# Up-product sums scaled out of PSUM by ScalarE, with the bias added by GpSimd, in place of one VectorE operation

## The reference

```python
# x = x + read(layernorm(x), ctx_1024)
q = query @ Wq.T + bq;  k = mem_state @ Wk.T + bk;  v = mem_state @ Wv.T + bv
scores = einsum('btd,bsd->bts', q, k) / sqrt(256)
# all but the 32 largest scores of a row are set to -inf
ctx = softmax(masked) @ v;   return ctx @ Wo.T + bo
# x = x + ffn(layernorm(x))
def bitlinear(x, w, b):
    xq = act_quant(rmsnorm(x))      # rounded to 8 bits by the row's largest value
    wq = weight_quant(w)            # rounded to -1, 0, 1 times the mean size
    return einsum('bsd,fd->bsf', xq, wq) + b
h = gelu(bitlinear(h, w1, b1));  return bitlinear(h, w2, b2)     # 256 -> 1024 -> 256
```

## Time and profile before

| | TensorE | VectorE | ScalarE | GpSimd |
|---|---|---|---|---|
| busy of the 300.1 us span | 278.8 | 242.7 | 207.7 | 128.4 |
| share | 93% | 81% | 69% | 43% |

### The profile page before, as it was taken

The page is one execution under the profiler, slowest core; times in us unless marked ns, Lnnn a source line. Parts: engine busy times, 40 slices in busy tenths (PEclk is TensorE's granted clock), DMA queues, the critical chain, the costliest instruction groups (busy, mean ns, idle before and its releaser), DMA issues. The chain is left out here.

```text
span 300.1 us, 5613 instructions
## 1 busy us (share of the span) xinstructions
PE 278.8 (93%) x1640; PEld 243.7 (81%) x1640; DVE 242.7 (81%) x1000; ACT 207.7 (69%) x319; POOL 128.4 (43%) x211
## 2 busy tenths in 40 slices
PE   7999998999999999999999999999999989959735
PEld 7989997998778977898789888978897879838424
DVE  2563799798889988998899888998897888965761
ACT  1559586355489658965896579667976697474871
POOL 4025773603924292529342935194419131504020
PEclk9999999999999999999999999999999999998957
DMA  7971010001000101010101010101000100100001
GB/s 238 303 272 37 3 35 1 21 0 52 4 17 0 56 0 52 3 54 2 54 0 55 1 52 2 54 3 52 2 20 0 54 2 18 36 2 1 32 3 37
DMA packets 12461, 12.25 MB, mean 41 GB/s; under 512 B 3597, under 2 KB 11342, under 8 KB 12430
## 3 DMA queue, kind: packets, MB, share of 16 engines
q1 hardware_dynamic: 11726, 10.83, 11.2%
q0 software_dynamic: 272, 0.79, 1.2%
q10 hardware_dynamic: 432, 0.26, 0.3%
HBM read 9.77 MB, written 2.10 MB: 40 GB/s over the span
## 5 line engine op out<-in xcount | busy, mean ns | idle before, releaser
L393 PE MATMUL bank<-vo,pT 128*128 128x257 f32 (+1 forms) x416 | 98.3, 385 | 0.0
L393 PEld LDWEIGHTS bank<-vo,pT 128*128 128x128 f32 (+1 forms) x416 | 77.2, 192 | 10.7 <-issue 0.2
L1352 DVE MAX8 cand<-s_sb 128x8 f32<-128x50 f32 (+1 forms) x512 | 62.0, 201 | 5.8 <-ACT s_sb L999 5.6
L999 ACT ACTIVATE s_sb<-score 128x400 f32<-128x400 f32 x64 | 31.5, 501 | 28.7 <-PE score L241 28.7
L241 PE MATMUL score<-k_high,q_low 128*128 128x400 f32 (+1 forms) x128 | 50.7, 396 | 0.0
L241 PE MATMUL score<-k_low,q_high 128*128 128x400 f32 (+1 forms) x128 | 44.2, 346 | 0.0
L241 PE MATMUL score<-k_high,q_high 128*128 128x400 f32 (+1 forms) x128 | 44.1, 344 | 0.0
L1049 ACT ACTIVATE pT<-bank 128x512 f32<-128x512 f32 x64 | 32.9, 516 | 12.5 <-PE bank L249 12.5
L249 PE MATMUL bank<-ident,e_all 128*128 128x128 f32 (+1 forms) x208 | 33.0, 275 | 8.1 <-ACT pT L1049 6.9
L249 PEld LDWEIGHTS bank<-ident,e_all 128*128 128x128 f32 (+1 forms) x208 | 24.7, 141 | 15.0 <-issue 11.2
L1387 DVE SCALAR_TENSOR_TENSOR e_all<-s_sb,best,e_all 128x1601 f32<-128x1601 f32 x16 | 32.5, 2033 | 3.1 <-ACT e_all L1041 3.1
(11 more groups left out here) (141 smaller groups left out, 529.9 us busy)
## 6 DMA issues: line engine op xcount, KB each, us to landing
x_in<-in_x SPq DMA_DIRECT2D x16, 128.0 KB, 2.2
w_sb<-in_L_ffn_w SPq DMA_DIRECT2D x2, 1024.0 KB, 14.3
x_res<-in_x SPq DMA_DIRECT2D x16, 128.0 KB, 2.0
out<-o_sb SPq DMA_DIRECT2D x16, 128.0 KB, 2.0
ctx_sb<-in_ctx SPq DMA_DIRECT2D x3, 512.0 KB, 5.6
b_bc<-in_L_ffn_b POOLq DMA_DIRECT2D x1, 512.0 KB, 9.3
w_q<-in_L_xattn_Wq SPq DMA_DIRECT2D x1, 256.0 KB, 3.0
w_k<-in_L_xattn_Wk ACTq DMA_DIRECT2D x1, 256.0 KB, 4.7
```

The lines of the kernel that those rows point to most:

```text
L393: ins = pe.matmul(bank[:, 0:DV], pT[0:n, t % 2, b * P:(b + 1) * P], vo[0:n, b, :], start=(b == 0), stop=(b == SB - 1))
L999: act.activation(s_sb[:, t % 2, at:at + n], score[c][:, 0:n], ACT.Copy).then_inc(s_copied, 1)
L1352: ins = dve.max(cand[:, t % 2, k:CAND:PIECES], s_sb[:, t % 2, k * PIECE:end])
```

## The change

`hidden` moves from VectorE to ScalarE. There it is an activation with a scale for each row, without the bias. A new GpSimd step `add_bias` adds the bias in place, and `gelu` waits for that by a new semaphore `biased` instead of for the bank. 32 operations leave VectorE, 32 come to ScalarE and 32 to GpSimd. The bank of `up` is free once ScalarE has read it.

```diff
@@ -853,6 +823,12 @@
                 pool.tensor_tensor(row2[:, t // 2 % 2, 1, u:u + 1], row2[:, t // 2 % 2, 0, u:u + 1], minus_half[:, 0:1],
                                    ALU.pow).then_inc(last2_step[u], 1)
 
+            def add_bias(t, h):
+
+                u, part = t % 2, slice(h * BANK, (h + 1) * BANK)
+                wait_drained(pool, ("up", t, h))
+                pool.tensor_tensor(g[:, u, part], g[:, u, part], b1_bc[:, part], ALU.add).then_inc(biased, 1)
...
@@ -1063,10 +1043,22 @@
                 take(("y1", t), y1T[:, :, u * P:(u + 1) * P], two_parts(("y1", t))[:, :, u * P:(u + 1) * P],
                      bias=unmagic_col[:, 0:1])
 
+            def hidden(t, h):
+
+                j, u = t // 2, t % 2
+                if t < LAST:
+                    act.wait_ge(row1_step, (j + 1) * ROW1)
+                else:
+                    act.wait_ge(last1_step[u], ROW1)
+                if t >= 2:
+                    act.wait_ge(y2_ready, t - 1)
+                src = wait_full(act, ("up", t, h))
+                drain(act.activation(g[:, u, h * BANK:(h + 1) * BANK], src[:, :], ACT.Copy, scale=row1[:, j % 2, 6, u:u + 1]),
+                      ("up", t, h))
+
             def gelu(t):
 
-                for h in range(2):
-                    wait_drained(act, ("up", t, h))
+                act.wait_ge(biased, 2 * t + 2)
                 act.activation(g[:, t % 2, :], g[:, t % 2, :], ACT.Gelu).then_inc(g_ready, 1)
 
             def squares(t):
...
@@ -1509,19 +1508,6 @@
                 dve.wait_ge(g_max_ready, t + 1)
                 tile_scales(row2, t // 2 % 2, u, last2_step[u], g_max[:, u:u + 1], wmean[:, 1:2])
 
-            def hidden(t, h):
-
-                j, u = t // 2, t % 2
-                if t < LAST:
-                    dve.wait_ge(row1_step, (j + 1) * ROW1)
-                else:
-                    dve.wait_ge(last1_step[u], ROW1)
-                if t >= 2:
-                    dve.wait_ge(y2_ready, t - 1)
-                src = wait_full(dve, ("up", t, h))
-                drain(dve.scalar_tensor_tensor(g[:, u, h * BANK:(h + 1) * BANK], src[:, :], row1[:, j % 2, 6, u:u + 1],
-                                               b1_bc[:, h * BANK:(h + 1) * BANK], ALU.mult, ALU.add), ("up", t, h))
-
             def gelu_max(t):
 
                 u = t % 2
@@ -1561,115 +1547,126 @@
```

The calls of all engines are put in a new order. The diff of these lists is long; a few of its lines stand here, of GpSimd's round:

```diff
+            for r in range(7):
+                if live(r - 1):
+                    residual(2 * r - 2)
+                if live(r):
+                    split_queries(r)
+                if live(r - 1):
+                    residual(2 * r - 1)
+                if live(r - 2):
+                    add_bias(2 * r - 4, 0)
+                    add_bias(2 * r - 4, 1)
+                    add_bias(2 * r - 3, 0)
...
+                    keep_residual(r - 2, 1)
+                    add_bias(2 * r - 3, 1)
```

More of the change, by code:

```diff
@@ L486, in _ @@
             scores(1, 2)
[L487 to L492, removed]
+            for r in range(7):
+                if r == 0:
+                    project_values(6)
+                if live(r):
+                    scores(2 * r + 1, 3)
+                if live(r - 2):
+                    turn_y2(2 * r - 3, 0)
+                    turn_y2(2 * r - 3, 1)
+                    down(2 * r - 4)
+                if live(r):
+                    turn_weights(2 * r, 0)
                 if live(r - 2):
@@ L520, in _ @@
                 if live(r + 1):
-                    scores(2 * r + 2, 2)
+                    scores(2 * r + 2, 3)
                 if live(r):
@@ L1633, in _ @@
                 if live(r):
-                    best_8(2 * r + 1, 0)
-                    next_8(2 * r + 1, 1)
                     next_8(2 * r + 1, 2)
-                if live(r + 2):
-                    ln1_stats(r + 2)
-                if live(r):
                     next_8(2 * r + 1, 3)
+                    count(2 * r + 1)
+                    attended(2 * r)
+                    weigh(2 * r + 1)
+                    largest_count(2 * r + 1)
+                    release(2 * r + 1)
+                    moments(2 * r)
+                if live(r + 1):
+                    candidates(2 * r + 2, 0)
+                if live(r - 1):
+                    gelu_max(2 * r - 2)
+                if live(r + 1):
+                    candidates(2 * r + 2, 1)
+                    candidates(2 * r + 2, 2)
+                    candidates(2 * r + 2, 3)
+                if live(r - 1):
+                    gelu_max(2 * r - 1)
+            centre(10)
+            best_8(12, 0)
+            next_8(12, 1)
+            next_8(12, 2)
+            next_8(12, 3)
+            count(12)
+            weigh(12)
+            attended(11)
+            largest_count(12)
+            moments(11)
+            release(12)
+            centre(11)
+            candidates(13, 0)
+            output(8)
+            candidates(13, 1)
+            candidates(13, 2)
+            candidates(13, 3)
+            best_8(13, 0)
+            next_8(13, 1)
+            output(9)
+            next_8(13, 2)
+            next_8(13, 3)
             count(13)
+            attended(12)
             weigh(13)
-            attended(12)
             largest_count(13)
-            hidden(10, 0)
+            moments(12)
+            centre(12)
             release(13)
-            hidden(10, 1)
-            hidden(11, 0)
             candidates(14, 0)
-            hidden(11, 1)
             gelu_max(10)
@@ L1666, in _ @@
             largest_count(14)
-            candidates(15, 0)
             moments(13)
@@ L1670, in _ @@
             centre(13)
+            candidates(15, 0)
+            output(10)
             candidates(15, 1)
-            output(10)
             candidates(15, 2)
@@ L1713, in _ @@
             tile_scales_2(15)
+            output(13)
             output(14)
```

462 lines of the change are left out of this document (199 added, 263 removed).

## The result

The changed kernel takes 298.60 us (median, 297.14 to 299.49) against 300.48 us (299.64 to 301.70) for the kernel before beside it. The ratio is 0.9935, with a 95% interval from 0.992 to 0.995: 0.65% faster, where 302.6 us, slower than before, was forecast. The profiled execution has a span of 296.5 us (own time 298.09). It lies 0.5 us under its median and the profiled one of before (301.79) 1.3 over its own, so the two traces differ by 3.6 us where the medians differ by 1.9.

The account below looks back on a forecast made before the run. TensorE's own work was taken to bound the middle. Opening -0.3, six periods +1.3 and end +1.7 sum to +2.7 us on the median 299.92: 302.6 us, own range 301.0 to 304.6, 8 in 10 295.5 to 305.5.

Parts of the forecast that it names:

- Added up from 5.2: table load 1.30: ScalarE's queue in a pair: after the second addition, table load 1.30 us, then Gelu and copies, first pT copy at 8.70.
- the signs named for "right": First additions about 2.4 us, others 1.28, starting inside a masking; TensorE waits for pT and y2; period 30.4 to 30.5.
- The waits: TensorE's new waits in a pair: 0.15 and 0.66 for pT copies, 0.48 for quantise_2; 1.3 us replacing 1.08.
- +0.4 a pair: Rise of the middle's period if each ScalarE scaling takes 682 ns; with the chosen 600 ns it was +0.2 us.
- The opening: TensorE's first turn of weights comes 0.2 to 0.4 us sooner: -0.3 us, bounds -1 and +1.
- The end: Last up products followed by a scaling and four GpSimd additions: +1.0, plus 0.7 for the clock; +1.7 us, from -0.7 to +3.
- the half clock: TensorE granted 1.2 instead of 2.4 GHz after idle time near the end: +1.7 us if on the path, 0.7 taken.
- over 8 us behind: Sign at the end: tile 15's pT copy starts over 8 us behind the last pair's first up product.
- an overlap that the forecast had the wrong way round: At the end, tile 15's masking starts at about 2.5, ahead of the second addition, which ends at 5.7; weights released about 5.1.
- The additions come free: Rival: second addition done at 4.2, waits shrink to about 0.3 a pair, middle -4.8 us; 294.9 us, chance 0.25.
- slack: Rival: additions collide but ScalarE has slack; waits stay 1.08 a pair, middle gives nothing, end +0.7; 300.3 us, chance 0.18.

Follow-up runs that it names:

- e1: Changed kernel with one more, always-over wait ahead of the Gelu, so the table load stands behind the wait for `biased`: 307.59 us, ratio to before 1.0201.
- e5: Changed kernel without GpSimd's 32 additions (bias b1 left out), the Gelu waiting for ScalarE's own scaled copy: 294.66 us, ratio to before 0.9771.
- e7: Changed kernel with the last two tiles (14 and 15) scaled and biased in one VectorE operation as before: 295.64 us, ratio to before 0.9821.
- e2: Kernel before with one wait ahead of the Gelu in place of two, so the table load runs ahead of the wait: 294.19 us, ratio 0.9788.

## Why the prediction was wrong

*Step that failed: "Added up from 5.2: table load 1.30".* The forecast took the place of the load from the earlier trace rows, behind the wait, and carried it over to a Gelu with another kind of wait. There it overlaps with the addition. The forecast's Gelu starts at 5.2 + 1.30 = 6.5, the measured one at 4.88; 1.3 of these 1.6 us are the load, the other 0.3 the second addition, done at 4.8 instead of 5.1. e1 puts the load back, alone, and gives 307.6 us, on the forecast's side of before; so the sign hung on 1.3 us per pair that the page of before could not show, but the order of the instructions with their waits did.

*The rest of the middle.* The collision and the starting times of the additions came as forecast: the signs named for "right" were there without the period that should go with them. The waits came only with the load behind (e1), two of three at the forecast's places: 1.6 us a pair in sum, as the period against that of e5 shows (30.63 - 29.06), where the forecast had 1.3. The period rose by 0.37 over before (30.26 to 30.63), and the forecast had +0.2 with a scaling of 600 ns and "+0.4 a pair" with 682; it was 685. ScalarE came to 85% of the middle (153.63 of 180 us), not to 81. The term that I chose was the wrong one of two: the price of a scaling was that of the copy with a column. The Trainium skill, ScalarE: Activation LUTs, "What ACT_TABLE_LOAD costs", states that each pointer operand of 128x1 adds about 93 ns to an ACTIVATE; the trace agrees (685 against 600), and that sentence would have settled the choice.

*The opening.* Forecast -0.3, measured -2.0; the eleven traces put the first up product at 80.3 to 80.8 in the old opening (three kernels) and at 78.2 to 79.6 in the new one (eight), about -1.5. The waits of 0.9, 0.6 and 0.5 shown above shrink to 0.6 in sum. I had followed only the first turn of weights and taken less than half of its wait, and nothing of the others.

*The end.* Forecast +1.7 (up to +3), measured +3.8. The direction and the place were right: scalings and four additions on one engine with little beside them. Missing was that two of tile 15's short VectorE steps were held until an addition ended (1.4 us longer together than in e7). TensorE's longer idle time met the half clock again, for which the forecast had 0.7. The pT copy of tile 15, "over 8 us behind" in the forecast, came at 6.3. The load explains little of that: in e1, with the load behind the wait, it comes at 6.7. The rest is an overlap that the forecast had the wrong way round. It let the masking of tile 15 in ahead of the second addition; measured, the masking starts at 3.2 instead of 2.5, when the second addition already runs, and takes 2.24 us. So the second addition is over sooner than forecast (at 3.8, not 5.7), and TensorE turns tile 15's weights later (at 5.6, not 5.1):

```profile
257.76 2.24 DVE L1386 SCALAR_TENSOR_TENSOR e_all<-s_sb,best,e_all 128x1601 f32<-128x1601 f32 x1
255.78 5.35 POOL L830 TENSOR_TENSOR g<-g,b_bc 128x512 f32<-128x512 f32 x3 [4.31 <-ACT g L1056]
```

*The rivals.* None of them is what happened. ScalarE had no slack: 1.34 us more at its Gelu cost 1.26 us a period (e1), and 0.27 less gave 0.31 (e5). "The additions come free" has the right size of the middle (-4.8 against -5.4) by a wrong mechanism: the additions did collide, and what vanished from the path was the load. Two independent changes came in one edit, the form of a wait and the split with its new order: the one gives 2.1% (e2), the other takes 1.5%.

## What to carry to other kernels

Where an engine switches activation tables, give the first instruction of the new table one wait only, for the event that comes last; in these kernels the load of 1.28 us then lies inside that wait. Look for ACT_TABLE_LOAD rows with an idle time in front: each is a place to try this, and here it gave 2% by one line. And when a change alters how an instruction waits, compare the order of instructions with the waits on them before costing anything else. Compare the split with the best version without it, too: no version with the split beats e2. Even e7, which has the split only where the middle covers the handovers, has a ratio to before of 0.9821 against 0.9788: not faster, with intervals that overlap.

## What the runs showed of the hardware

- A copy of a 128x512 bank with a scale column takes 685 ns, the plain one 600; the Gelu starts 0.01 us behind the table load's end in e2 (170.91 + 1.28 against 172.20).
- A GpSimd addition with two SBUF inputs holds up even a VectorE product of one column (1.21 us beside a sum of 512 columns, 0.67 beside one of 256, 0.15 with neither) and a VectorE rounding with a single tensor input (1.19 instead of 0.34). The other way, the masking of 1601 columns delays the addition that begins 0.67 us behind it: about 2.3 us instead of 1.27. The Trainium skill, SBUF — State Buffer, "🔬 SBUF: two separate sides", describes this lock, by which the one that starts first keeps the other out for its whole length; the traces agree, to within 0.15 us. It names two SBUF inputs and the two-port modes of VectorE; in which mode the rounding ran, no trace shows.
- A delay can set the period one for one while the profile prints no wait of the engine that pays: in the changed kernel TensorE is busy for 178.88 of 180 us, and 0.27 us less at the Gelu still took 0.31 off each period. The wait shows only in the starts, 0.43 us between two matmuls that follow each other in 0.18 without it.
